# A transformer block with self and cross attention: one maximum and one exponential per visit for two heads, and a new table of places

## The reference

```python
x_norm = modulate(_ln(x), shift_a, scale_a)
q, k, v = jnp.split(x_norm @ W_qkv + b_qkv, 3, axis=-1)
attn_w = jax.nn.softmax(jnp.einsum('bhqd,bhkd->bhqk', q, k) * scale, axis=-1)
attn_out = jnp.einsum('bhqk,bhkd->bhqd', attn_w, v)
x = x + gate_a[:, None] * (attn_out @ W_proj + b_proj)
q_c = _ln(x) @ W_qc + b_qc
k_c, v_c = jnp.split(_ln(context) @ W_kvc + b_kvc, 2, axis=-1)
x = x + softmax_attention(q_c, k_c, v_c) @ W_cproj + b_cproj
x_norm2 = modulate(_ln(x), shift_m, scale_m)
h = jax.nn.gelu(x_norm2 @ W_mlp1 + b_mlp1) @ W_mlp2 + b_mlp2
x = x + gate_m[:, None] * h
```

## Time and profile before

| | us |
|---|---|
| median of 3 runs | 1541.66 (1538.27 to 1548.11) |
| profiled execution, its own time | 1557.84 |
| its span (first to last instruction) | 1555.7 |
| PE busy | 1395.6, 90% |
| DVE busy | 1125.6, 72% |
| ACT busy | 1126.4, 72% |
| POOL busy | 720.7, 46% |

### The profile page before, as it was taken

The page is one execution under the profiler, slowest core; times in us unless marked ns, Lnnn a source line. Parts: engine busy times, 40 slices in busy tenths (PEclk is TensorE's granted clock), DMA queues, the critical chain, the costliest instruction groups (busy, mean ns, idle before and its releaser), DMA issues.

```text
span 1555.7 us, 40219 instructions
## 1 busy us (share of the span) xinstructions
PE 1395.6 (90%) x15090; PEld 913.7 (59%) x15090; DVE 1125.6 (72%) x2477; ACT 1126.4 (72%) x2373; POOL 720.7 (46%) x1005
## 2 busy tenths in 40 slices
PE   3576899999999999999999999989999999999775
PEld 1333466666666666666666666656666666655444
DVE  4657878878887778777887877767888777765511
ACT  3254778877887888877777888877787788877541
POOL 2233255455554545445555454544555455435432
PEclk8779999999999999999999999999999999999878
DMA  5122323323332332223333333223332333222110
GB/s 178 59 73 77 94 83 98 87 87 102 104 101 89 95 94 88 91 92 97 100 101 102 91 96 98 86 76 92 103 101 87 87 103 90 88 74 78 50 43 15
DMA packets 142051, 138.03 MB, mean 89 GB/s; under 512 B 38241, under 2 KB 116226, under 8 KB 141858
## 3 DMA queue, kind: packets, MB, share of 16 engines
q1 hardware_dynamic: 141858, 135.45, 28.7%
HBM read 56.60 MB, written 9.57 MB: 43 GB/s over the span
## 4 chain that ended last, share of the span: by engine, by line
PE 47%; DMA 18%; DVE 12%; SPq 7%; ACT 7%; issue 5%; POOL 4%; POOLq 0%; DVEq 0%; ACTq 0%
PE dense_ps L408 10%; PE dense_ps L410 9%; PE dense_ps L409 9%; DMA o_rb_cross<-r_dram_cross 9%; PE max_ps L696 6%; PE o_ps L731 6%; SPq L493 5%; PE exp_ps L713 4%; DMA r_dram_cross<-o_r_cross 4%; DVE mx_cross L1050 4%; DVE mx_self L1050 3%; ACT probs L854 3%; DMA o_d_self<-o_sb_self 2%; PE dense_ps L638 2%; POOL o_n_cross L1156 2%
## 5 line engine op out<-in xcount | busy, mean ns | idle before, releaser
L854 ACT ACTIVATE probs<-exp_ps 128x512 f32<-128x512 f32 x1024 | 561.4, 609 | 159.9 <-PE exp_ps L713 157.2
L1050 DVE TENSOR_REDUCE mx_cross<-max_ps 128x2 f32<-128x512 f32 x512 | 328.7, 684 | 91.1 <-PE max_ps L696 88.2
L1050 DVE TENSOR_REDUCE mx_self<-max_ps 128x2 f32<-128x512 f32 x512 | 326.6, 680 | 39.7 <-PE max_ps L696 38.3
L1189 POOL TENSOR_TENSOR g_split<-G,g_split 128x512 f16<-128x512 f32 x128 | 146.6, 1159 | 87.1 <-ACT g_split L842 87.1
L408 PE MATMUL dense_ps<-mlp_hi,g_split 128*128 128x256 f16 x512 | 144.3, 282 | 12.3 <-POOL g_split L1189 12.3
L1156 POOL TENSOR_TENSOR o_n_self<-o_n_self,o_rb_self 128x512 f32<-128x512 f32 x32 | 40.5, 1267 | 247.0 <-DMA o_rb_self<-r_dram_self 247.0
L408 PE MATMUL dense_ps<-xt,mlp_hi 128*128 128x256 f16 x512 | 141.5, 276 | 3.0 <-DVE xt L1013 2.8
L410 PE MATMUL dense_ps<-mlp_hi,g_split 128*128 128x256 f16 x512 | 143.3, 280 | 0.0
L409 PE MATMUL dense_ps<-mlp_lo,g_split 128*128 128x256 f16 x512 | 143.3, 280 | 0.0
L409 PE MATMUL dense_ps<-xt,mlp_hi 128*128 128x256 f16 x512 | 141.1, 276 | 0.0
L410 PE MATMUL dense_ps<-xt,mlp_lo 128*128 128x256 f16 x512 | 141.0, 275 | 0.0
(11 more groups left out here) (213 smaller groups left out, 3343.0 us busy)
## 6 DMA issues: line engine op xcount, KB each, us to landing
k_stack_self<-split_k SPq DMA_DIRECT2D x192, 64.0 KB, 2.6
...
```

The source lines that it names most:

```text
L854: nc.scalar.activation(probs[:, (t + ab) % 8], exp_ps[:, ab], ACT.Exp).then_inc(exp_taken[kind], 1)
L1050: nc.vector.tensor_reduce(mx[kind][:, :, ab, t // 2], max_ps[:, ab].rearrange("p (q k) -> p q k", q=2), AX_X, ALU.max).then_inc(max_taken[ ...
L1189: nc.gpsimd.tensor_tensor(g_split[:, 1, 2 * i:2 * i + 2], G[:, 2 * i:2 * i + 2], g_split[:, 0, 2 * i:2 * i + 2], ALU.subtract).then_inc(g_ ...
```

## The change

A maxima visit ends with one reduction over both banks and an exponentials visit with one exponential over both, each waiting for the second bank and signalling twice. The table of places is new: `PLAN`, `BANK` (qc and vc to bank 0, cproj and t1 to bank 2) and `AHEAD`, which now corrects batches 0, 1, 2, 28 to 31.

```diff
-    "load_x": (-2, 1, 14), "ln1": (-1, 0, 0), "norm1": (-1, 0, 5), "t1": (-1, 0, 9), "t1_hi": (-1, 0, 9),
+    "load_x": (-2, 1, 13), "ln1": (-1, 0, 0), "norm1": (-1, 0, 6), "t1": (-1, 0, 8), "t1_hi": (-1, 0, 9),
...
-                    for ab in range(2):
-                        act.wait_ge(exp_ready[kind], b.n * TILES + t + ab + 1)
-                        nc.scalar.activation(probs[:, (t + ab) % 8], exp_ps[:, ab], ACT.Exp).then_inc(exp_taken[kind], 1)
+                    act.wait_ge(exp_ready[kind], b.n * TILES + t + 2)
+                    nc.scalar.activation(probs[:, t % 8:t % 8 + 2], exp_ps[:], ACT.Exp).then_inc(exp_taken[kind], 2)
...
-                    for ab in range(2):
-                        dve.wait_ge(max_ready[kind], b.n * TILES + t + ab + 1)
-                        nc.vector.tensor_reduce(mx[kind][:, :, ab, t // 2],
-                                                max_ps[:, ab].rearrange("p (q k) -> p q k", q=2), AX_X, ALU.max
-                                                ).then_inc(max_taken[kind], 1)
+                    dve.wait_ge(max_ready[kind], b.n * TILES + t + 2)
+                    nc.vector.tensor_reduce(mx[kind][:, :, :, t // 2].rearrange("p q a -> p a q"),
+                                            max_ps[:].rearrange("p a (q k) -> p a q k", q=2), AX_X, ALU.max
+                                            ).then_inc(max_taken[kind], 2)
```

More of the change, by code:

```diff
@@ L40 @@
[L40 to L44, removed]
@@ L50 @@
-    "o_norm_cross": (4, 0, 2), "o_hi_cross": (4, 0, 3), "o_lo_cross": (4, 0, 5), "cproj": (4, 0, 6),
[5 rows of a table removed]
-    "y": (5, 0, 5), "y_add": (5, 0, 5), "store": (6, 0, 1),
+    "k": (-1, 1, 2), "k_hi": (-1, 1, 2), "k_lo": (-1, 1, 6), "stack_k": (-1, 1, 6), "v": (-1, 1, 11),
+    "v_hi": (-1, 1, 11), "split_self": (0, 0, 15), "m_self": (0, 1, 1), "m_copy_self": (0, 1, 2),
+    "o_gather_self": (1, 0, 11), "o_recip_self": (1, 0, 12), "r_out_self": (1, 0, 15), "r_back_self": (1, 1, 1),
+    "o_norm_self": (1, 1, 1), "o_hi_self": (1, 1, 3), "o_lo_self": (1, 1, 4), "rows_a": (0, 1, 1),
@@ new lines @@
+    "xr": (0, 1, 13), "proj": (1, 1, 6), "x2": (1, 1, 9), "x2_add": (1, 1, 12), "ln2": (1, 1, 13),
+    "norm2": (2, 0, 1), "t2": (2, 0, 2), "t2_hi": (2, 0, 2), "t2_lo": (2, 0, 3), "qc": (2, 0, 5),
+    "qc_hi": (2, 0, 5), "qc_lo": (2, 0, 6), "stack_qc": (2, 0, 8), "xc": (2, 0, 9), "load_c": (0, 0, 7),
+    "lnc": (0, 1, 3), "normc": (0, 1, 8), "tc": (1, 0, 7), "tc_hi": (1, 0, 15), "tc_lo": (1, 1, 0),
+    "kc": (1, 1, 3), "kc_hi": (1, 1, 14), "kc_lo": (2, 0, 2), "stack_kc": (2, 0, 7), "vc": (2, 0, 11),
@@ L57 @@
+    "vc_hi": (2, 0, 11), "split_cross": (2, 1, 15), "m_cross": (3, 0, 0), "m_copy_cross": (3, 0, 1),
+    "o_gather_cross": (3, 1, 11), "o_recip_cross": (3, 1, 12), "r_out_cross": (3, 1, 12),
+    "r_back_cross": (3, 1, 14), "o_norm_cross": (4, 0, 3), "o_hi_cross": (4, 0, 3), "o_lo_cross": (4, 0, 4),
[6 rows of a table added]
 }
 BANK = {
-    "m_self": 0, "m_cross": 2, "qc": 2, "cproj": 0, "tc": 1, "kc": 0, "t3": 0, "mlp1_0": 0, "mlp1_1": 2,
-    "mlp1_2": 1, "mlp1_3": 2, "vc": 2, "t1": 0, "proj": 2, "mlp2": 1, "q": 2, "k": 1, "v": 1, "t2": 2,
+    "m_self": 0, "m_cross": 2, "qc": 0, "cproj": 2, "tc": 1, "kc": 0, "t3": 0, "mlp1_0": 0, "mlp1_1": 2,
@@ L62 @@
+    "mlp1_2": 1, "mlp1_3": 2, "vc": 0, "t1": 2, "proj": 2, "mlp2": 1, "q": 2, "k": 1, "v": 1, "t2": 2,
 }
 AHEAD = {
[L65 to L80, removed]
[4 rows of a table removed]
[L85 to L90, removed]
[4 rows of a table removed]
[L95 to L98, removed]
[3 rows of a table removed]
@@ L102 @@
[L102 to L106, removed]
[3 rows of a table removed]
-        "y_add": -3, "store": 23},
@@ L122 @@
-    30: {"max_cross": 2, "ln1": -1, "stack_q": 6, "stack_k": -2, "v_hi": 1, "split_self": -1, "m_self": -1,
-        "m_copy_self": -1, "o_gather_self": 1, "o_recip_self": -2, "r_out_self": -5, "r_back_self": -3,
-        "o_norm_self": -1, "o_lo_self": -1, "rows_a": -16, "xr": -7, "proj": -4, "x2": -3, "x2_add": 1, "ln2": 1,
-        "norm2": 5, "t2": 2, "t2_hi": 2, "t2_lo": 1, "qc": 2, "qc_hi": 3, "qc_lo": -1, "stack_qc": -1, "xc": -3,
-        "load_c": 10, "lnc": 2, "normc": -8, "tc": -5, "tc_hi": -1, "tc_lo": -1, "kc": 1, "kc_hi": -1, "kc_lo": 3,
-        "stack_kc": -3, "vc": 3, "vc_hi": 1, "split_cross": 3, "m_cross": 1, "m_copy_cross": 1,
-        "o_recip_cross": 3, "r_out_cross": 1, "r_back_cross": 3, "o_norm_cross": 1, "o_hi_cross": -1,
[4 rows of a table removed]
-        "store": -12},
@@ L134 @@
-    31: {"max_self": -2, "max_cross": 1, "exp_cross": -1, "load_x": -4, "ln1": -6, "norm1": -3, "t1": -1,
-        "t1_hi": -1, "q": 1, "q_hi": 2, "q_lo": 1, "stack_q": 3, "k": 4, "k_hi": 3, "k_lo": 7, "stack_k": -3,
-        "v": 8, "split_self": -3, "m_self": -1, "m_copy_self": -1, "o_gather_self": -1, "o_recip_self": -2,
-        "r_out_self": -5, "r_back_self": -3, "o_norm_self": -1, "rows_a": -9, "xr": -23, "proj": -1, "x2": -1,
-        "x2_add": 4, "ln2": 3, "norm2": 1, "t2": 1, "t2_hi": 1, "qc": -1, "stack_qc": -4, "xc": -2, "load_c": -7,
-        "lnc": -22, "normc": -21, "tc": -1, "tc_hi": -3, "tc_lo": -1, "kc_hi": -3, "kc_lo": 1, "stack_kc": -5,
-        "vc": 1, "split_cross": -4, "m_cross": -3, "m_copy_cross": -4, "o_gather_cross": -38,
-        "o_recip_cross": -34, "r_out_cross": -34, "r_back_cross": -31, "o_norm_cross": -29, "o_hi_cross": -29,
[4 rows of a table removed]
-        "y_add": -77, "store": -51},
+    0: {"exp_self": -1, "load_x": 9, "ln1": 12, "norm1": 18, "t1": 8, "t1_hi": 8, "t1_lo": 8, "q": 8, "q_hi": 7,
+        "q_lo": 7, "o_gather_self": 1, "o_recip_self": -1, "t2_hi": -1, "xc": 1, "normc": -2, "kc_hi": -1,
+        "vc_hi": -5, "mlp2_0": 1, "store": -5},
@@ new lines @@
+    1: {"load_x": 8, "ln1": 8, "norm1": 8, "t1": 8, "t1_hi": 7, "t1_lo": 7, "q": 9, "q_hi": 10, "q_lo": 8,
+        "k": 10, "r_out_self": 1, "r_back_self": 3, "o_norm_self": 3, "load_c": 3, "tc_hi": 2, "tc_lo": 1,
+        "o_gather_cross": 1, "g_hi_1": -2, "g_lo_3": 1, "y": 1, "y_add": 1},
+    2: {"m_self": 1, "tc": -3, "stack_kc": 5, "g_hi_3": 1, "g_lo_2": -5, "g_lo_3": -4, "mlp2_0": -2},
+    28: {"mlp2_3": 2},
+    29: {"t1": -1, "v": 1, "o_gather_cross": 1, "o_recip_cross": 2, "r_out_cross": -3, "r_back_cross": -1,
[4 rows of a table added]
+        "y_add": -1},
@@ L147 @@
+    31: {"max_cross": 2, "exp_cross": 8, "k": -1, "k_hi": -1, "r_back_self": 1, "qc_lo": 1, "normc": 4,
+        "split_cross": 2, "m_cross": 3, "m_copy_cross": 4, "o_gather_cross": 7, "o_recip_cross": 8,
[4 rows of a table added]
 }
```

13 lines of the change are left out of this document (removed), and 45 rows, old and new, of tables (AHEAD, PLAN).

## The result

| | before | after |
|---|---|---|
| median of 4 runs, us | 1542.43 (1538.27 to 1548.11) | 1520.28 (1515.87 to 1522.56) |
| profiled execution, its own time | 1557.84 | 1521.74 |

The ratio is 0.9842, with a 95% interval from 0.982 to 0.9865: 22 us or 1.6% less (17.5 were forecast). The two profiled executions differ by 36 us (23 were forecast), since that of before was 15 us above its median and that of after only 1.5. Beside the later experiments the kernel before had medians of 1549.4, 1550.3 and 1552.0 us; there the comparisons are ratios to it. Two later executions, of 1980 and 5926 us, showed a granted clock of 0.65 and 0.22 and are in no comparison.

A forecast was written before the change was run, and what follows sets the result against it. PE's own matmul stream was taken to bound the middle. Terms -14 (cross chain), -3 (clock), -4, -2.3, -0.8 (merge), +2 (fill), -1 (tail) sum to -23.1; allowing for unprofiled runs, 17.5 off the 1541.7 median gives 1524 us, range 1503 to 1549.

The forecast's parts named there:

- PE's own stream bounds the middle: From 275 to 1400 us PE's unchanged matmuls set the pace; only 38 us of waits could be had there.
- Cross chain, 14 of 19.8 us: Middle: cross reciprocals' trip through DRAM 1.0 us sooner by SP's new order, cutting PE's waits for exponentials by 14 us.
- Clock, 3 us: Middle: shorter PE stalls avoid a lower granted clock (0.93 over 49 us in the bad batch), gaining 3 us.
- The merge, 7.1 us: Merged instructions save 0.07 us a reduction and 0.04 an exponential where PE waits: 4 middle, 2.3 fill, 0.8 end.
- the later start costs nothing: Maxima and exponentials visits: waiting for the second bank adds no time, as the two halves' matmuls run side by side.
- Maxima in the middle, -4: From 275 to 1400 us, 65 PE waits for DVE's maxima (18.2 us) shrink by 4 us through merged reductions.
- Fill up to 275 us, +2 -2.3 = -0.3: Batch 1's copy of turned maxima behind q's and tc's splits costs 2 us; merged reductions at 33 waits save 2.3.
- Tail, -1.8: From 1400 us: merged instructions save 0.8 us, and mlp2 in place of mlp1 in exponential visits saves 1.
- all of the 16 us are the chain's: If the profiled run's extra 16 us are all cross-chain stalls absent without profiling, the change brings some 10 us; if none, 23.
- The stalls didn't stay: Rival, 0.25: the cross output lands as late as now because the fetch itself is slow; only merges count, 1536 us.
- POOL's new place of Y's addition: Rival, 0.15: Y's addition ahead of norm1 on POOL makes PE wait for xn unless the cross chain is sooner; 1553 us.
- PE had no room: Rival, 0.03: PE's true load is 59%, so DVE and ACT bound the kernel and 36 us come off each; 1505 us.

The follow-up runs named there:

- the self side: The kernel before with SP's rows_b alone moved in batches 3 to 21, from directly ahead of o_d_self to behind the cross fetch: ratio 0.9954.
- The cross side alone: The kernel before with three SP steps moved in batches 3 to 21 (Ctx load behind turned maxima, output's store and rows_a behind self fetch): ratio 0.9886.
- the pair of runs: The changed kernel with two reductions and two exponentials a visit again, ratio 0.9817, beside the changed kernel itself, 0.9807.

## Why the prediction was right, point by point

**PE's own stream bounds the middle: right.** The matmuls are the same, and in the new table DVE's and ACT's lighter load moved nothing that can be told; 42.0 us a batch is what is left.

**Cross chain, 14 of 19.8 us: right in place; the size is near, in part by luck.** 5.2 us are left over the same 1125 us (7 times), 14.6 less. But 19.8 is the most that any profile with the old order has: with the merge alone it is 10.1, with the self side 4.1 and 9.4 more for the turned maxima. The chain from reciprocal to multiplication went from 9.40 to 8.39, the 1.0 us of the forecast. Most of it, 0.9, lies between store and fetch (the store's landing fell from 2.5 to 1.8 us, not to 1.5). The 0.5 in the fetch (medians of parts needn't add up to that of the whole) is no more than the spread, since with the same order it took 6.50 us before and 6.15 with the merge alone. The cross side alone shows the chain as cause.

**Clock, 3 us: 5 to 6.** I counted the one dip of the bad batch. PE's busy time for the same work in the middle fell by 6.0 us; there was another dip behind a stall at 500 us (timeline of PE, before):

```profile
500.31 0.61 PE L713 MATMUL exp_ps<-q_stack_cross,k_stack_cross 50*128 50x256 f16 x4 [2.18 <-ACT probs L854]
```

The stretches before, 498 to 506 us, and after, 500 to 506 us:

```profile
498.00:506.00 8.00, 5.82 (x52) 3.40 (x48) 5.63 (x11) 5.00 (x11) 3.90 (x7) 0.79 0.22 67
```

```profile
500.00:506.00 6.00, 6.00 (x77) 3.60 (x74) 5.06 (x11) 5.83 (x11) 0.87 (x2) 1.00 0.43 118
```

The 8 us at 0.79 and the 49 at 0.93 are 1.7 and 3.4 us short of the full clock. The runs with the merge alone and with the cross side alone have no such dip between 275 and 1400 us, so other executions need not have them.

**The merge, 7.1 us: wrong.** It brought 5.5 us with the old table, but in the new table, for which it was forecast, a ratio of about 0.001 (under 2 us), not to be told from nothing. The instructions are as long as forecast (1.22 and 1.03 us), but "the later start costs nothing" failed. The visit of the fill that answers to the earlier trace rows, at the same clock, DVE and then PE:

```profile
56.35 1.23 DVE L986 TENSOR_REDUCE mx_self<-max_ps 128x4 f32<-128x1024 f32 x1 [0.81 <-PE max_ps L634]
```

```profile
57.63 0.61 PE L634 MATMUL max_ps<-k_stack_self,q_stack_self 48*128 48x256 f16 x4 [1.42 <-DVE mx_self L986]
```

DVE idles 0.81 us before the reduction in place of 0.70, as it waits for the second bank, and PE's gap is 1.42 us, not 1.31 and not even 1.38. The run with the merge alone has such visits at both clocks (timeline of PE):

```profile
93.84 0.39 PE L696 MATMUL max_ps<-k_stack_self,q_stack_self 48*128 48x256 f16 x4 [0.42 <-DVE mx_self L1048]
95.66 0.61 PE L696 MATMUL max_ps<-k_stack_self,q_stack_self 48*128 48x256 f16 x4 [1.42 <-DVE mx_self L1048]
97.68 0.61 PE L696 MATMUL max_ps<-k_stack_self,q_stack_self 48*128 48x256 f16 x4 [1.42 <-DVE mx_self L1048]
```

From one visit's first matmul to the next it takes 2.02 us at the lower clock (before: 1.99) and 1.81 to 1.82 at the full one (before: 1.77 to 1.79). So a merged visit in a tight loop costs 0.03 to 0.04 us more. By the Trainium skill's rule that I weighed (VectorE: DVE Perf Modes, The DRAIN you can't avoid) each should have saved 0.125 us, an estimate from that page's cost table. The trace doesn't agree: the instruction is 0.07 us shorter than the pair. What the merge brought with the old table may have been on ACT, behind the late copy, where each exponential is 0.05 us shorter. That this is how isn't shown; that it is gone once the chain is early, the pair of runs shows.

**Maxima in the middle, -4: -6.8** (18.2 to 11.4 over 1125 us), but not by the merge: with it the old table has 22.1, and without it the new one has 7.5. That this term came near is luck.

**Fill up to 275 us, +2 -2.3 = -0.3: -5.9.** The first exponential of batch 1 is 2.9 us later, as forecast (106.02 against 103.08), but by batch 4 this is more than given back (-1.6), and the two batches behind bring 4.3 more; 3.7 of them are shorter waits of PE (8.5 to 4.8). It isn't one execution's chance: from batch 0's first self maxima to batch 6's the seven profiles with the old table take 221.6 to 226.8 us, the seven with the new one 216.0 to 220.0. Since the merge brings nothing here (its run takes 224.6 us, before 222.1), the places alone bring the 5.9, outside the bound of -4. Which places is open. **Tail, -1.8: -3.0.**

**The sum, -23.1: -35.7** in the profiled executions. By stretches of the same work: up to batch 6 -5.9 (forecast -0.3), the middle -26.8 (-21), the end -3.0 (-1.8); these make up the 12.6 us. By medians I took 17.5, near the middle between 10 ("all of the 16 us are the chain's") and 23 ("none"), which would be 16.5; it was 22, and 27 to 30 where the kernel before ran at 1550. So the forecast lies near the result for two reasons that offset each other: the merge's 7 us didn't come, and the places brought more in the fill, at the clock and in the middle's maxima than they were given. Whether the kernel before also spreads more from run to run isn't shown: where both ran side by side, its eleven runs lie within 11.7 us and five of the changed kernel within 8.7.

**The rivals.** The stalls didn't stay. POOL's new place of Y's addition costs 1.0 to 2.7 us of waits in the middle, none visible in the time; the longest is 0.3 us, just over the 0.2 that was to be a sign of it. That it decides only if the chain isn't sooner was its condition, and the chain was. PE had no room: 29 and 26 us less work on DVE and ACT (not 36 each) gave nothing that can be told.

What the rest of the table adds lies at the ends. Beside the cross side alone the changed kernel takes 5.4 us less up to batch 6 (221.6 to 216.2), 2.8 less in the middle (batches 6 to 29), where the cross side was moved in 19 batches only, and 3.4 less at the end (237.1 to 233.7), each from one execution. Which steps do it at the ends is open.
